# Mixture-of-experts stage after attention: rows of both choices are dispatched before the first expert tile, and first results return in 32 small pieces

## The chip, the cores and the metric

One core of a Trainium2 chip (trn2) runs the whole program. The metric is the device time of one execution in microseconds, as a median over runs. An execution under the hardware profiler gives the trace and has a time of its own.

## What is computed

The input is an image of 64 channels by 128 by 128 in float32. It is normalised along each row, goes through a gated attention layer with four heads (projection, softmax over the row, projection back) and is added to itself. Then each of the 8192 rows of 128 values is a token for a mixture of eight experts:

```python
def _L0_ffn_ref(x, Wg, bg, W1, b1, W2, b2):
    TOP_K = 2
    xf = x.reshape(-1, D)                        # 8192 tokens of D = 128
    gate_logits = xf @ Wg + bg
    top_w, top_i = jax.lax.top_k(gate_logits, TOP_K)
    top_w = jax.nn.softmax(top_w, axis=-1)
    w_dense = jnp.sum(jax.nn.one_hot(top_i, E, dtype=xf.dtype) * top_w[..., None], axis=1)
    out = jnp.zeros_like(xf)
    for e in range(E):
        h = jax.nn.gelu(xf @ W1[e] + b1[e], approximate=False)
        out = out + w_dense[:, e:e + 1] * (h @ W2[e] + b2[e])
    return out.reshape(B, L, D)
```

The tokens that enter are the layer-normalised rows, and the result is added to the rows themselves. Only the two chosen experts of a token count, so the kernel sends each token to two experts.

## The kernel before

**Up to the routing.** The first half of the span is the attention, which the change does not touch. Then VectorE (DVE) normalises the 64 rows that each partition holds into `pay` (L984), TensorE (PE) computes the gate logits, and VectorE works out for each choice k the row `pos[k]` at which each token goes (`route`, L1008). A token's payload is 128 values, its weight and its own number (528 bytes).

**Dispatch.** GpSimd (POOL) issues one indirect DMA per payload column: 128 tokens, one from each partition, are scattered to the buffer `routed[k]` in device memory (`scatter_rows`, L623). There are 64 of them for the first choice and 64 for the second. Both choices use the same `pay`; between them VectorE overwrites the weight column (L1091), which waits until the first 64 have landed and raises `meta_ready` to 2.

**Tiles.** Each choice is a slot of 39 tiles of 256 rows, sorted by expert, 78 tiles in all. Each tile goes through these steps: SyncE (SP) loads its rows (`load_rows`, L520, 132 KB) into one of 8 buffers; PE transposes them (L1304); ScalarE (ACT) and VectorE split them into a high and a low half-precision part (L792, L1099); PE multiplies by the first weights (L1314 to L1316); ACT applies the gelu (L801); VectorE splits its result (L1105, L1107); PE multiplies by the second weights (L1322 for the bias, L1330); ACT scales by the token's weight into `yo` (L809); POOL scatters the two halves of 128 rows to `expert_out[slot]` (`send_rows`, L627, two indirect DMAs at L630). The engines run staggered: in step s, PE transposes tile s+1, does the first products of tile s and the second products of tile s-1. The steps -1 to 4 are written out, the steps 5 to 44 are a loop of five iterations with eight steps in its body, the steps 45 to 76 a second loop of four iterations, and three steps are written out behind it (`tile_steps`, L386).

**Order on POOL.** All 64 first-choice scatters come first. Then, for each of the 39 tiles of slot 0, some second-choice scatters come ahead of `send_rows(t)`: eight ahead of tile 0, and from there 56 spread over 31 tiles, by this line:

```python
due = [LEAD + (HALF - LEAD) * t // (SLOT_TILES - 8) for t in range(SLOT_TILES)]
```

Slot 1 has the sends alone. `send_rows(t)` waits for `y_ready`.

**Order on SP.** SP waits until the first-choice scatters have landed, and issues the loads of slot 0. The load of tile t waits for the send of tile t-8, whose buffer it takes. Then SP waits for the second-choice scatters and loads the first eight tiles of slot 1. Once slot 0 is sent, it loads the first choice's results from `expert_out[0]` into `shared` in four chunks of 16 rows per partition, two DMAs of 512 KB each (L539), with eight tile loads between two chunks. VectorE adds them to `xt` four rows per partition at a time, once in every other step of the second loop (`add_first`, L1112), and waits for a chunk at its first quarter. After the last send come the second choice's results (L547, L1125) and the output (L551).

Of the kernel before, what the change touches and what calls it, by code (L numbers as in the profile page):

```python
# [50 lines left out]
def wait(engine, sem, value):  # L51

    if isinstance(value, int) and value <= 0:
        return
    engine.wait_ge(sem, value)
# [12 lines left out]

def build(nc, x, ln_w, ln_b, wq, wk, wv, wb, wg_w, wg_b, wrep_w, wrep_b, Wg, bg, W1, b1, W2, b2, out):
    _, C, H, W = x.shape  # L70
    NH = wb.shape[0]
    HC = wq.shape[0]
    D = HC // NH
    HALF = H // 2
    R = 4
# [3 lines left out]
    CH = 4  # L79
    CR = HALF // CH  # L80
    E, _, HID = W1.shape
    HB = HID // P
    TOKENS = C * H
    TILE = 256
    SLOT_TILES = TOKENS // TILE + E - 1
    TILES = 2 * SLOT_TILES
    ROW = W + 4
    IN_BUFS = 8
    YO_BUFS = 4
    B2_ROWS = 33  # L90
    WPIECE = E * HID // UNITS
    assert W == P and H == P and 2 * C == P and HC == P and UNITS % 2 == 0

    with ExitStack() as ctx:
        def sb(name, shape, dt=F32):
            return ctx.enter_context(nc.sbuf_tensor(name, shape, dt))
# [4 lines left out]
        def sem(name):  # L101
            return ctx.enter_context(nc.semaphore(name))
# [3 lines left out]
        shared = sb("shared", [P, HALF, W])  # L106
# [28 lines left out]
        b1_sb = sb("b1_sb", [P, E, HB])  # L135
        b2_row = sb("b2_row", [B2_ROWS, E * P])
        wg_sb = sb("wg_sb", [P, E])
# [69 lines left out]
        def sbm(name, shape, dt=F32):  # L207
            return ctx.enter_context(nc.sbuf_tensor(name, shape, dt))
# [3 lines left out]
        w_l = [sbm(f"w{n}_l", [P, E, HB, P], F16) for n in (1, 2)]  # L212
        b2_parts = sbm("b2_parts", [B2_ROWS, E, HB, P], F32R)
        ones_x = sbm("ones_x", [B2_ROWS, P], F32R)
        rows_all = sbm("rows_all", [P, IN_BUFS, 2, ROW])
# [20 lines left out]
        hl = [sbm(f"hl{p}", [P, HB, TILE], F16) for p in range(2)]  # L236
        yo = [sbm(f"yo{b}", [P, 2, P]) for b in range(YO_BUFS)]
        pay_place = pay[:].bitcast(I32)[:, :, W + 1]
# [87 lines left out]
        scattered = [sem(f"scattered{k}") for k in range(2)]  # L326
# [9 lines left out]
        y_full = sem("y_full")  # L336
        y_ready = sem("y_ready")
        y_sent = [sem(f"y_sent{b}") for b in range(YO_BUFS)]
        y0_in = sem("y0_in")
        y0_added = sem("y0_added")  # L340
        y_in = [sem(f"y_in{c}") for c in range(CH)]
        y_added = sem("y_added")
# [3 lines left out]
        lwv = ln_w.rearrange("c (f i) j -> f c i j", f=2)  # L346
        lbv = ln_b.rearrange("c (f i) j -> f c i j", f=2)
        outv = out[0].rearrange("c (f i) j -> f c i j", f=2)

        LEAD = 8  # L350

        def chunk(c):
            return slice(c * CR, (c + 1) * CR)
# [29 lines left out]
        BODY = 8  # L383
# [29 lines left out]
        def sent_count(b, t):  # L413

            return 32 * ((t - b) // YO_BUFS + 1) if t >= b else 0

# [50 lines left out]
        def _(sp):  # L467
# [29 lines left out]
            sp.wait_ge(const_ready, 1)  # L497
            for row in (0, B2_ROWS - 1):
                sp.dma_start(b2_row[row:row + 1, :], b2.rearrange("(o e) d -> o (e d)", o=1)).then_inc(small_in, 16)
# [13 lines left out]
            outputs_v = [e[0:TOKENS].rearrange("(c f i) w -> f c i w", f=2, i=HALF) for e in expert_out]  # L513

            def sent_through(t):

                for b in range(YO_BUFS):
                    wait(sp, y_sent[b], sent_count(b, t))

            def load_rows(t):  # L520
                slot, n = divmod(t, SLOT_TILES)
                wait(sp, y_sent[t % YO_BUFS], sent_count(t % YO_BUFS, t - IN_BUFS))
                sp.dma_start(rows_in[t % IN_BUFS], routed_v[slot][n]).then_inc(rows_loaded[t % IN_BUFS], 16)

            LATER = SLOT_TILES + IN_BUFS
            sp.wait_ge(scattered[0], 16 * HALF)
            for t in range(SLOT_TILES):
                load_rows(t)
            sp.wait_ge(scattered[1], 16 * HALF)
            for t in range(SLOT_TILES, LATER):  # L530
                load_rows(t)

            sent_through(SLOT_TILES - 1)
            for c in range(CH):
                if c:
                    for t in range(LATER + BODY * (c - 1), LATER + BODY * c):
                        load_rows(t)
                for f in range(2):
                    sp.dma_start(shared[f * C:(f + 1) * C, chunk(c), :], outputs_v[0][f, :, chunk(c), :]).then_inc(y0_in, 16)  # L539
            for t in range(LATER + BODY * (CH - 1), TILES):  # L540
                load_rows(t)

            sent_through(TILES - 1)
            sp.wait_ge(y0_added, HALF // R)
# [10 lines left out]
        def _(pool):  # L555
# [67 lines left out]
            def scatter_rows(k, i):  # L623
                pool.indirect_dma_start(routed[k], bass.IndirectOffsetOnAxis(ap=pos[k][:, i:i + 1], axis=0),  # L624
                                        pay[:, i, :], None).then_inc(scattered[k], 16)

            def send_rows(t):  # L627
                pool.wait_ge(y_ready, t + 1)
                for k in range(2):
                    pool.indirect_dma_start(  # L630
                        expert_out[t // SLOT_TILES],
                        bass.IndirectOffsetOnAxis(ap=row_place[t % IN_BUFS][:, k, W + 1:W + 2], axis=0),
                        yo[t % YO_BUFS][:, k, :], None).then_inc(y_sent[t % YO_BUFS], 16)

# [2 lines left out]
                scatter_rows(0, i)  # L637

            pool.wait_ge(meta_ready, 2)
            due = [LEAD + (HALF - LEAD) * t // (SLOT_TILES - 8) for t in range(SLOT_TILES)]  # L640
            for t in range(SLOT_TILES):
                for i in range(due[t - 1] if t else 0, min(HALF, due[t])):
                    scatter_rows(1, i)
                send_rows(t)
            for t in range(SLOT_TILES, TILES):
                send_rows(t)

        @block.scalar
# [169 lines left out]
        def _(dve):  # L818
            chain = Chain(dve, dve_step)

            for c in range(CH):
# [8 lines left out]
                k = chunk(c)  # L830
# [22 lines left out]
            for c in range(CH):  # L853
                k = chunk(c)
# [25 lines left out]
            for f in range(2):  # L880
                k = slice(f * C, (f + 1) * C)
# [194 lines left out]

            chain.link(nc.vector.tensor_scalar(b2_row[:], b2_row[:], hscale[0:B2_ROWS, 1:2], hscale[0:B2_ROWS, 2:3], ALU.mult, ALU.mult))
            b2_e = b2_row[:].rearrange("o (e d) -> o e d", e=E)
            chain.link(nc.vector.tensor_copy(b2_parts[:, :, 0, :], b2_e))
            lo = slice(B2_ROWS - 1, B2_ROWS)  # L1080
            chain.link(nc.vector.tensor_tensor(b2_parts[lo, :, 0, :], b2_e[lo], b2_parts[lo, :, 0, :], ALU.subtract))
# [29 lines left out]

            def add_first(g, j):  # L1112

                if j == 0:
                    dve.wait_ge(y0_in, 32 * g + 32)
                k = bass.ds(g * CR + j * R, R)
                nc.vector.scalar_tensor_tensor(xt[:, k, :], shared[:, k, :], y_scale[:, 0:1], xt[:, k, :],
                                               ALU.mult, ALU.add).then_inc(y0_added, 1)

            tile_steps(dve, tile_step, add_first)  # L1120

            dve.wait_ge(y0_added, HALF // R)
# [237 lines left out]
```

## Time and profile before

| what | value |
|---|---|
| runs | 1155.31 to 1161.32 us, median 1159.59 us (3 runs) |
| the profiled execution's own time | 1150.0 us |
| its span | 1148.2 us, mean granted TensorE clock 0.827 |
| PE, DVE, ACT, POOL busy | 62%, 66%, 54%, 39% of the span |
| bytes moved | 70.39 MB, mean 61 GB/s |
| chain that ended last | PE 35%, DVE 26%, issue 26%, ACT 4%, DMA 4% |

Times in the profile count from the start of the span. A row of a timeline is one instruction, or several merged, with its start, its length, and in brackets the idle time of its engine before it and what ended that. "issue" is idle time of an engine in which it waited for nothing that the profile shows; "remote" is a release that the profile can't place. PE is the multiplying, PEld the loading of weights into the array. The granted clock is a share of 2.4 GHz: 0.5 is 1.2 GHz.

### The profile page before, as it was taken

What the parts mean: (1) busy time and instruction counts of PE and PEld (TensorE: products, weight loads), DVE (VectorE), ACT (ScalarE), POOL (GpSimd) and SP (SyncE); (2) the same over time, 40 slices, a digit from 0 to 9 for tenths busy, and PEclk for the clock granted to TensorE, in tenths of its full rate; (3) what the DMA queues carried; (4) which work ended last, traced back from release to release, by engine and by line L of the source; (5) the groups of instructions that cost most, each with busy time, mean ns of one, the idle gap of its engine ahead of it and who ended that gap; (6) DMA issues with size and microseconds to landing.
All of it is one profiled execution on the core that took longest, in us unless ns stands there. A gap on an engine that the chain in (4) does not pass through costs nothing.

```text
span 1148.2 us, 24693 instructions
## 1 busy us (share of the span) xinstructions
PE 710.1 (62%) x7641; PEld 541.2 (47%) x7642; DVE 758.4 (66%) x2465; ACT 615.8 (54%) x1531; POOL 445.3 (39%) x492
## 2 busy tenths in 40 slices
PE   0036888888888888739500025757675777797760
PEld 0003666666666666625300014545554565676650
DVE  4795899999999999975484004334443455686653
ACT  0024898898888889816412014434443465576550
POOL 3001243434334343310058763555554643454350
PEclk9996899999999999958755556877787788898885
DMA  9735999900000000000001121211121213432219
GB/s 203 173 73 153 165 26 167 18 0 0 0 0 0 0 0 0 0 1 0 1 33 39 53 83 38 57 54 56 56 58 51 65 54 85 108 92 76 77 57 276
DMA packets 102861, 70.39 MB, mean 61 GB/s; under 512 B 52645, under 2 KB 93158, under 8 KB 99752
## 3 DMA queue, kind: packets, MB, share of 16 engines
q1 hardware_dynamic: 92392, 42.65, 24.5%
q0 software_dynamic: 9152, 18.89, 5.0%
q10 hardware_dynamic: 1280, 8.39, 3.2%
q8 instruction: 18, 0.29, 0.1%
q14 instruction: 19, 0.16, 0.1%
HBM read 36.04 MB, written 33.61 MB: 61 GB/s over the span
## 4 chain that ended last, share of the span: by engine, by line
PE 35%; DVE 26%; issue 26%; ACT 4%; DMA 4%; another core or an unknown queue 1%; POOL 1%; SPq 1%; DVEq 0%; ACTq 0%; POOLq 0%
PE PT L1330 11%; DVE L L919 6%; DVE pl L909 4%; PE S L1314 3%; PE S L1316 3%; PE S L1315 3%; PE PT L1322 2%; DMA xt<-in_x 2%; DVE rowstat L442 2%; DVE xt L944 2%; DMA shared<-expert_out 2%; PE S L1148 1%; PE A L1171 1%; PE PT L1196 1%
## 5 line engine op out<-in xcount | busy, mean ns | idle before, releaser
L630 POOL DMA_INDIRECT expert_out<-yo,rows_all x156 | 158.8, 1018 | 200.8 <-ACT yo L809 162.3
L801 ACT ACTIVATE hf<-S,b_sb,inv_hscale 128x256 f32<-128x256 f32 x312 | 153.7, 567 | 72.8 <-remote 42.8
L624 POOL DMA_INDIRECT routed<-pay,pos x128 | 132.3, 1034 | 121.4 <-DVE pay L1059 81.1
L712 ACT ACTIVATE L<-L,lmin 128x128 f32<-128x128 f32 x512 | 159.2, 390 | 0.4
L919 DVE CUSTOM_DVE_ANT_0 L<-S,biasN,logit_scale 128x128 f32<-128x128 f32 x512 | 148.4, 345 | 2.5 <-issue 1.9
L1105 DVE TENSOR_SCALAR hh<-hf,hscale 128x512 f16<-128x512 f32 x156 | 77.5, 497 | 87.9 <-ACT hf L801 64.5
L607 POOL TENSOR_TENSOR og<-gt,on 128x256 f32<-128x256 f32 x64 | 46.5, 727 | 229.3 <-DVE on L932 229.3
L1107 DVE SCALAR_TENSOR_TENSOR hl<-hf,hscale,hh 128x512 f16<-128x512 f32 x156 | 117.4, 753 | 5.6
L792 ACT ACTIVATE fx_h<-A 128x256 f16<-128x256 f32 x39 | 14.9, 383 | 183.3 <-PE A L1304 68.4
L1330 PE MATMUL PT<-w_h,hh 128*128 x624 | 91.6, 229 | 16.3 <-issue 10.7
L1304 PE MATMUL A<-identity,rows_all 128*128 128x128 f32 x78 | 18.3, 323 | 134.4 <-DMA rows_all<-routed 72.3
L1314 PE MATMUL S<-fx_h,w_h 128*128 128x256 f16 x312 | 97.9, 314 | 5.2 <-issue 4.9
L1330 PE MATMUL PT<-w_h,hl 128*128 x624 | 91.5, 228 | 13.7 <-issue 13.7
L1315 PE MATMUL S<-fx_l,w_h 128*128 128x256 f16 x312 | 98.1, 314 | 2.3 <-issue 2.3
L1316 PE MATMUL S<-fx_h,w_l 128*128 128x256 f16 x312 | 97.8, 313 | 1.5 <-issue 1.3
L1330 PE MATMUL PT<-w_l,hh 128*128 x624 | 90.5, 227 | 7.8 <-issue 7.8
L707 ACT ACTIVATE ph<-PT 128x512 f16<-128x512 f32 x128 | 76.0, 594 | 25.5 <-PE B L1213 13.3
L1099 DVE TENSOR_TENSOR fx_l<-A,fx_h 128x256 f16<-128x256 f32 x39 | 16.4, 422 | 104.1 <-ACT fx_h L792 66.1
L1196 PE MATMUL PT<-identity,L 128*128 128x128 f32 x512 | 83.0, 301 | 3.2 <-DVE pl L909 2.5
L909 DVE TENSOR_TENSOR pl<-PT,ph 128x512 f16<-128x512 f32 x128 | 82.8, 682 | 2.1 <-ACT ph L707 2.1
L1304 PEld LDWEIGHTS A<-identity,rows_all 128*128 128x128 f32 x78 | 9.0, 160 | 136.2 <-issue 136.1
L1196 PEld LDWEIGHTS PT<-identity,L 128*128 128x128 f32 x512 | 64.5, 155 | 8.1 <-DVE pl L909 2.9
(235 smaller groups left out, 2085.7 us busy)
## 6 DMA issues: line engine op xcount, KB each, us to landing
rows_all<-routed SPq DMA_DIRECT2D x78, 132.0 KB
routed<-blank SPq DMA_DIRECT2D x2, 5031.0 KB, 41.6
shared<-expert_out SPq DMA_DIRECT2D x16, 512.0 KB, 11.4
xt<-in_x SPq DMA_DIRECT2D x8, 512.0 KB, 24.6
shared<-in_L_conv_ln_w ACTq DMA_DIRECT2D x8, 512.0 KB, 11.8
shared<-in_L_conv_ln_b ACTq DMA_DIRECT2D x8, 512.0 KB, 10.4
out<-xt SPq DMA_DIRECT2D x8, 512.0 KB, 9.7
expert_out<-yo,rows_all POOLq DMA_INDIRECT x156
```

The costliest lines, as they stand in the source:

```text
L624: pool.indirect_dma_start(routed[k], bass.IndirectOffsetOnAxis(ap=pos[k][:, i:i + 1], axis=0), pay[:, i, :], None).then_inc(scattered[k], 16)
L630: pool.indirect_dma_start(expert_out[t // SLOT_TILES], bass.IndirectOffsetOnAxis(ap=row_place[t % IN_BUFS][:, k, W + 1:W + 2], axis=0), yo ...
L712: last = nc.scalar.activation(L[p][:, h, i, :], L[p][:, h, i, :], ACT.Exp, scale=-1.0, bias=lmin[p][:, h * R + i:h * R + i + 1])
L801: last = nc.scalar.activation(hf[p][:, b, :], S[2 * p + pair][:, k * TILE:(k + 1) * TILE], ACT.Gelu, scale=inv_hscale[:, 0:1], bias=b1_fla ...
L909: nc.vector.tensor_tensor(pl[i % 2][:], PT[i % 2][:], ph[i % 2][:], ALU.subtract).then_inc(pl_ready, 1)
L919: last = nc.vector.tensor_tensor_reduce(out=L[p][:, h, i, :], in0=S[h][:, i * P:(i + 1) * P], in1=biasN[:, h, :], scale=logit_scale[:, 0:1 ...
L1107: nc.vector.scalar_tensor_tensor(hl[p][:, b, :], hf[p][:, b, :], hscale[:, 2:3], hh[p][:, b, :], ALU.mult, ALU.subtract).then_inc(hl_ready, 1)
L1196: last = nc.tensor.transpose(PT[i % 2][:, h * P:(h + 1) * P], L[p][:, h, i, :], identity[:])
L1314: nc.tensor.matmul(dst, w1_h[:, block_at], fx_h[p][:], start=True, stop=False)
L1315: nc.tensor.matmul(dst, w1_h[:, block_at], fx_l[p][:], start=False, stop=False)
L1316: last = nc.tensor.matmul(dst, w1_l[:, block_at], fx_h[p][:], start=False, stop=True)
L1330: last = nc.tensor.matmul(PT[p][:, k * P:(k + 1) * P], h_part[p][:, b, k * P:(k + 1) * P], w_part[:, block_at], start=False, stop=b == HB ...
```

## The change

All 128 scatters are issued ahead of the first send, and SP waits for all of them before it loads the first tile. `LEAD` and `due` go. The four chunks of first results become 16 pieces of 4 rows per partition, two DMAs of 128 KB each. Piece g is issued behind the load of tile 46 + 2g, and waits until piece g-2 was added. VectorE waits for each piece.

```diff
+    FIRST_BACK = 46
...
-        y0_in = sem("y0_in")
+        y0_in = [sem(f"y0_in{k}") for k in range(2)]
...
-
-        LEAD = 8
...
-            LATER = SLOT_TILES + IN_BUFS
+            def load_first(g):
+                wait(sp, y0_added, g - 1)
+                for f in range(2):
+                    sp.dma_start(shared[f * C:(f + 1) * C, g * R:(g + 1) * R, :],
+                                 outputs_v[0][f, :, g * R:(g + 1) * R, :]).then_inc(y0_in[g % 2], 16)
+
             sp.wait_ge(scattered[0], 16 * HALF)
-            for t in range(SLOT_TILES):
+            sp.wait_ge(scattered[1], 16 * HALF)
+            for t in range(TILES):
                 load_rows(t)
-            sp.wait_ge(scattered[1], 16 * HALF)
-            for t in range(SLOT_TILES, LATER):
-                load_rows(t)
-
-            sent_through(SLOT_TILES - 1)
-            for c in range(CH):
-                if c:
-                    for t in range(LATER + BODY * (c - 1), LATER + BODY * c):
-                        load_rows(t)
-                for f in range(2):
-                    sp.dma_start(shared[f * C:(f + 1) * C, chunk(c), :], outputs_v[0][f, :, chunk(c), :]).then_inc(y0_in, 16)
-            for t in range(LATER + BODY * (CH - 1), TILES):
-                load_rows(t)
+                if t >= FIRST_BACK and (t - FIRST_BACK) % 2 == 0 and (t - FIRST_BACK) // 2 < HALF // R:
+                    if t == FIRST_BACK:
+                        sent_through(SLOT_TILES - 1)
+                    load_first((t - FIRST_BACK) // 2)
...
-            due = [LEAD + (HALF - LEAD) * t // (SLOT_TILES - 8) for t in range(SLOT_TILES)]
-            for t in range(SLOT_TILES):
-                for i in range(due[t - 1] if t else 0, min(HALF, due[t])):
-                    scatter_rows(1, i)
-                send_rows(t)
-            for t in range(SLOT_TILES, TILES):
+            for i in range(HALF):
+                scatter_rows(1, i)
+            for t in range(TILES):
                 send_rows(t)
...
             def add_first(g, j):
 
-                if j == 0:
-                    dve.wait_ge(y0_in, 32 * g + 32)
+                dve.wait_ge(y0_in[j % 2], 64 * g + 32 * (j // 2) + 32)
```

## Rows read from the trace of the kernel before

**Rows 1.** Stretches (columns: us; PE, PEld, DVE, ACT, POOL busy; clock; DMA; GB/s)
```profile
715.50:771.79 56.29, 36.12 (x313) 27.63 (x313) 22.03 (x40) 22.18 (x56) 30.75 (x32) 0.80 0.21 60
771.79:824.50 52.71, 36.53 (x312) 27.12 (x313) 23.33 (x40) 22.70 (x56) 30.27 (x30) 0.76 0.19 56
...
881.20:929.27 48.07, 34.23 (x312) 26.38 (x313) 23.31 (x40) 22.80 (x56) 24.58 (x24) 0.78 0.20 56
929.27:966.30 37.03, 28.71 (x312) 23.48 (x313) 22.03 (x40) 22.41 (x56) 15.92 (x16) 0.91 0.34 86
966.30:1002.56 36.26, 28.55 (x312) 23.72 (x313) 25.00 (x44) 22.63 (x56) 16.44 (x16) 0.88 0.36 90
1002.56:1039.18 36.62, 29.16 (x313) 24.32 (x313) 24.83 (x44) 22.63 (x56) 16.34 (x16) 0.87 0.33 87
1039.18:1074.81 35.63, 28.07 (x312) 23.43 (x313) 24.71 (x44) 22.63 (x56) 16.33 (x16) 0.93 0.35 89
```

**Rows 2.** Timeline of PE, two stops in a tile and one at a loop's head
```profile
707.07 0.22 PE L1330 MATMUL PT<-w_h,hl 128*128 x1 [1.09 <-issue]
708.47 0.27 PE L1330 MATMUL PT<-w_h,hl 128*128 x1 [1.18 <-issue]
...
966.30 0.69 PE L1304 MATMUL A<-identity,rows_all 128*128 128x128 f32 x2 [6.72 <-issue]
```

**Rows 3.** Timeline of POOL, first and last of a burst, and the last second-choice scatter
```profile
699.65 1.46 POOL L630 DMA_INDIRECT expert_out<-yo,rows_all  x1 [15.39 <-ACT yo L809]
...
707.73 0.95 POOL L624 DMA_INDIRECT routed<-pay,pos  x1 [0.30 <-issue]
...
909.15 0.96 POOL L624 DMA_INDIRECT routed<-pay,pos  x1 [0.30 <-issue]
```

**Rows 4.** Chain that ended last, in order of time, pieces of the loops (start, us)
```profile
936.30 1.45 PE PT L1330 x24
939.59 1.45 PE PT L1330 x24
...
1062.39 1.74 PE PT L1330 x24
1066.48 1.50 PE PT L1330 x24
```

**Rows 5.** Timeline of POOL, first-choice scatters and the eight behind them
```profile
582.94 1.11 POOL L624 DMA_INDIRECT routed<-pay,pos  x1 [81.09 <-DVE pay L1059]
...
609.92 5.20 POOL L624 DMA_INDIRECT routed<-pay,pos  x1 [0.30 <-issue]
...
671.57 0.96 POOL L624 DMA_INDIRECT routed<-pay,pos  x1 [0.30 <-issue]
674.40 0.96 POOL L624 DMA_INDIRECT routed<-pay,pos  x1 [1.87 <-issue]
...
683.23 1.03 POOL L624 DMA_INDIRECT routed<-pay,pos  x1 [0.31 <-issue]
```

**Rows 6.** Timeline of DVE, the rewriting of the weight column
```profile
673.90 0.22 DVE L1091 COPY pay<-weight 128x64 f32<-128x64 f32 x1 [55.21 <-DMA routed<-pay,pos]
```

**Rows 7.** Timeline of SP's queue
```profile
673.89 274.76 SPq L523 DMA_DIRECT2D rows_all<-routed  x47
...
1058.40 1.12 SPq L539 DMA_DIRECT2D shared<-expert_out  x2
```

**Rows 8.** Timeline of PE, the written-out steps
```profile
676.32 0.66 PE L1304 MATMUL A<-identity,rows_all 128*128 128x128 f32 x2 [72.27 <-DMA rows_all<-routed]
...
688.24 0.55 PE L1322 MATMUL PT<-b_parts,ones_x 33*128 x1 [4.39 <-issue]
692.20 0.39 PE L1330 MATMUL PT<-w_h,hh 128*128 x2 [3.41 <-DVE hl L1107]
```

**Rows 9.** Timeline of ACT, the second pair of tile 0's gelus
```profile
689.73 1.02 ACT L801 ACTIVATE hf<-S,b_sb,inv_hscale 128x256 f32<-128x256 f32 x2 [6.83 <-remote]
```

**Rows 10.** DMA issues of the page: size of one, median us to landing
```profile
shared<-expert_out SPq DMA_DIRECT2D x16, 512.0 KB, 11.4
```

## The prediction

> **What bounds the kernel now.** I read the chain of waits, then the table of stretches, then the timelines of PE and POOL. Only the expert stage, from 673.9 us, is touched. Its bulk is a loop whose iterations are eight steps, so the table cuts it at PE's first transpose of each iteration [rows 1]. All iterations have the same 312 or 313 matmuls, but the first takes 56.3 us, the second 52.7, the third again over 50 and the fourth 48.1, and the next four 37.0, 36.3, 36.6 and 35.6. The reader is to see what else differs: POOL has 24 to 32 instructions in the first four and 16 in the others, and the granted clock is 0.76 to 0.80 against 0.87 to 0.93. DMA moves more in the last four (86 to 90 GB/s against 56 to 60), so it is not bytes that slow the others.
>
> PE's timeline shows how the time goes: inside one group of products, where no wait on an engine stands, PE stops for 1.1 us at a time, put down to "issue" [rows 2]. Beside it lies POOL's timeline: from 699.65 to 708.7 it issues seven indirect DMAs with some 0.3 us between them, sends and scatters mixed, and the two stops fall at the end of that burst [rows 3]. With the last second-choice scatter at 909.15 [rows 3] the stops end, still in slot 0: the tiles behind it pass every 3.29 us [rows 4]. So the slowdown belongs to the second-choice scatters among the sends, not to slot 0, and PE is starved of instructions while POOL's DMAs stand close. That POOL's packets hold up PE's instruction fetch is my reading; the rows show only that both coincide.
>
> Ahead of the loop there is a second bound: VectorE stands 55.2 us for the first-choice scatters [rows 6]. They are serial on POOL [rows 5], and the first tile waits for them.
>
> **Part 1: the second scatters ahead of the tiles.** Before, the last first-choice scatter starts at 671.57, SP issues its first load at 673.89 (2.32 us later) and the first second-choice scatter starts at 674.40 [rows 5, 7]. The eight up to 683.23 start 8.83/7 = 1.261 us apart [rows 5]. After, 64 stand in a row: 63 x 1.261 = 79.5, so the last starts at 753.9 and has landed at 756.2. SP's first load moves from 673.9 to 756.2: **+82.3 us**. Nothing hides it: VectorE has nothing left to do ahead of the tiles but the weight column [rows 6], and every engine waits for the first tile. The first batch's pitch was (671.57 - 582.94)/63 = 1.407, because of a few long ones about 609.92 (5.20 us) [rows 5]; that would make this term 9.2 larger. I take 1.261, the pitch of the second-choice scatters themselves. No scatter comes closer, so the term's other end is 82.3 itself.
>
> **Part 2: the loop without scatters.** POOL has two sends per tile, as now in the last four iterations: 2 x 1.26 = 2.5 us in 3.29. The five iterations of the first loop take 966.30 - 715.50 = 250.8 us [rows 1]. The three of the second loop that the table ends on average 36.17; five of these are 180.9, so **-69.9 us**. By the shortest, 35.63, it would be -72.6; by the longest clean one, 37.03, -65.6. I take the mean, because each has one stop at the loop's head (6.72 us at 966.30 [rows 2]) that stays with or without scatters.
>
> **Part 3: the written-out steps.** PE starts at 676.32 and enters the loop at 715.50 [rows 1, 8]. The eight lead scatters (674.4 to 684.3 [rows 5]) fall on this start. Two stops of 1.09 and 1.18 us are of the kind found in the loop [rows 2]: 2.3 us go. Then PE stands 4.39 us on "issue" and 3.41 for VectorE, which waits for ACT, which stood 6.83 us between two pairs of gelus [rows 8, 9]. Without ACT's stop the second pair would follow at 682.9, VectorE's split would end at about 685.2, and PE would go on there and not at 692.2: 7.0 us. Whether this is the same starvation or first-pass code that is slow in any case no row tells. Bounds 2.3 and 9.3, the middle **-5.8 us**, since the rows near it speak for both.
>
> **Part 4: pieces for chunks.** The bytes are the same, and the last row loads and adds come in the same steps. A chunk disturbs the tile it falls on: the chunk at 1058.40 [rows 7] makes one tile 4.09 us and not 3.29 [rows 4], 0.8 us, and the second loop has three. Four pieces have the work of a chunk, so I take **0**; at best 3 x 0.8 = 2.4 are saved; at worst each of 16 pieces costs as a chunk does, 12.8 - 2.4 = +10.4. The new wait of SP (piece g waits for the add of piece g-2, VectorE's step 42 + 2g) holds back the row load of tile 47 + 2g, which PE transposes in step 46 + 2g: four steps, 13 us. Without it that load would wait for the send of tile 39 + 2g, which ACT writes in step 41 + 2g, so the new wait delays it by about one step. VectorE's wait for piece g comes in step 46 + 2g, also some 13 us behind its issue, and a pair four times as large lands in 11.4 us [rows 10]. Behind that wait stands the next tile's split, for which PE would wait. The 24 extra issues on SP and the 12 extra waits at the adds cost nothing, SP being idle between loads.
>
> The Trainium skill (DMA: Bandwidth & Descriptors, the measurements from device memory) has a rule against this part: put at least 1 MiB in a DMA to get 75% of peak. By that the 128 KB pieces are inefficient; the result would be the worst end just named. The row loads of 132 KB, one per 3.29 us without a wait on them in the last four iterations, speak against it here.
>
> **Sum**, against the profiled execution's own 1150.0 us: 82.3 - 69.9 - 5.8 + 0 = +6.6, so 1156.6. The median of the runs, 1159.59, lies 9.6 above that execution; the same difference on it gives **1166.2 us**. The tail (last results, last add, output) is unchanged. In short, most of what the interleaving costs now is what it hides: 75.7 us of slowdown against 82.3 of serial POOL time.
>
> **Rivals.**
> 1. Break-even. The price of starvation is all of what the bounds allow: 72.6 in the loop and 9.3 ahead of it, 81.9 together. Then 1159.6 + 0.4 = 1160.0. For it: a stop of both PE and ACT right at the lead scatters [rows 8, 9]. Against it: PE stops for 6.72 us at a loop's head without scatters too [rows 2].
> 2. Not slower but faster: ordinary runs starve more than the profiled one. The iterations with scatters differ by 4 us among themselves, those without by 1, so the 9.6 us between execution and median may lie there. If all of it does and goes, with break-even else: 1150.4. It decides once the runs' starvation exceeds the profiled by more than 6.2 us beyond rival 1. Against it: nothing locates the 9.6 us.
> 3. Pieces disturb one by one: the worst end of part 4, 1166.2 + 10.4 = 1176.6. For it: chunks do. Against it: row loads don't.
> 4. The pitch is 1.407 in the second batch as well: 1175.4.
> 5. The stops stay. The Trainium skill (Runtime: NRT & Kernel Launch, Instruction fetch mechanics) calls the crossing of an instruction block "mostly hidden". By that the 1.1 us stops would be something else, maybe slot 0's own. Worked out from rows: only +82.3 is left, 1241.9. The clean tiles of slot 0 behind 909 [rows 1, 4] speak strongly against it.
> 6. The change doesn't do what it says: the tiles would start before 756. SP's two waits at the head exclude it; no chance.
>
> **How the numbers follow.** Forecast 0.50, rival 1 0.22, rival 2 0.13, rival 3 0.07, rival 4 0.05, rival 5 0.03. A measurement of this kernel can tell about 0.5%, 5.8 us, from no change. The forecast's sum stands just past that bound (+6.6), and its terms spread by some 4 us either way, so of its 0.50 I give 0.34 to slower and 0.16 to same. Slower: 0.34 + 0.07 + 0.05 + 0.03 = 0.49. Same: 0.16 + 0.22 = 0.38. Faster: 0.13. The range runs from rival 2 to rival 3, 1150 to 1177; outside it lie rival 5 and the far parts of the others. The likeliest case's own range is 1161 to 1171.
>
> **What would show it.** First row load at 756 (part 1), scatters 1.26 us apart. Each iteration of the first loop at 35.6 to 37 us, with a clock near 0.9 and 16 POOL instructions (part 2). From PE's first transpose to the loop entry 30 to 37 us, not 39.2; ACT's stop of 6.8 us gone or not decides between forecast and rival 1 (part 3). No wait of VectorE on a DMA at the adds and iterations of the second loop at 36 (part 4). First load far from 756, or any first-loop iteration over 40 us, proves me wrong.

## The result and the profile after

The changed kernel takes 1176.07 us (median of 4 runs, 1173.98 to 1181.52), the kernel before beside it 1158.34 us (4 runs): ratio 1.016, 95% interval 1.0114 to 1.0207, so 1.6% slower. The forecast was slower, 1166.2 us in a range of 1150 to 1177.

The experiments will show that the answer depends on where a program runs. The kernel before took 1158 to 1161 us in the runs above and in one later set, 1154 in another, and 1068 in four other sets of runs, with no median between. A set's runs share one chip. I call the places with 1154 to 1161 **place A** and those with 1068 **place B**. What makes the difference no run tells. It may not be the chip alone: the second set of part 1 alone (place B, 1068.96) and, ten minutes later, the set of the last experiment (place A, 1153.79) bear the same chip number, 1; whether it names the same chip both times is not known.

The stretches of the expert stage after the change, cut as in [rows 1] at PE's first transpose of each iteration (columns: us, then busy time of PE, PEld, DVE, ACT, POOL with instructions, granted clock, DMA share, GB/s):

```profile
760.10:792.51 32.41, 21.23 (x173) 16.09 (x173) 14.42 (x26) 14.67 (x33) 5.83 (x6) 0.76 0.19 50
792.51:828.16 35.65, 28.91 (x312) 24.16 (x313) 22.63 (x40) 22.73 (x56) 16.53 (x16) 0.88 0.21 58
828.16:862.91 34.75, 28.40 (x313) 23.58 (x313) 22.45 (x40) 22.62 (x56) 16.15 (x16) 0.89 0.22 62
862.91:897.39 34.48, 27.98 (x313) 23.43 (x313) 22.48 (x40) 22.62 (x56) 16.17 (x16) 0.90 0.22 62
897.39:933.60 36.21, 29.35 (x312) 24.57 (x313) 22.49 (x40) 22.68 (x56) 16.14 (x16) 0.88 0.22 63
933.60:969.39 35.79, 28.43 (x312) 23.59 (x313) 22.71 (x40) 22.63 (x56) 16.21 (x16) 0.93 0.24 70
969.39:1010.14 40.75, 30.42 (x312) 24.45 (x313) 24.67 (x44) 22.09 (x56) 16.49 (x16) 0.88 0.29 78
1010.14:1051.51 41.37, 30.43 (x313) 24.61 (x313) 24.67 (x44) 22.08 (x56) 16.20 (x16) 0.87 0.27 75
1051.51:1092.04 40.53, 30.17 (x312) 24.40 (x313) 24.68 (x44) 22.09 (x56) 16.47 (x16) 0.88 0.28 79
```

The reader is to see two things. The five iterations of the first loop are at 34.5 to 36.2 us with 16 POOL instructions each, where the first four took 48.1 to 56.7. And the second loop, which before took 35.6 to 36.6 [rows 1], now takes 40.5 to 41.4, although DVE and ACT are busy for about the same time as before and PE for only 1.7 us more (30.3 for 28.6).

SP's queue after the change:

```profile
757.81 195.25 SPq L522 DMA_DIRECT2D rows_all<-routed  x47
953.23 1.15 SPq L527 DMA_DIRECT2D shared<-expert_out  x2
...
988.97 1.09 SPq L527 DMA_DIRECT2D shared<-expert_out  x2
990.11 2.24 SPq L522 DMA_DIRECT2D rows_all<-routed  x2
997.97 1.09 SPq L527 DMA_DIRECT2D shared<-expert_out  x2
```

The first row load stands at 757.81, not 673.89 [rows 7]. In the second loop each piece is issued with two row loads right behind it. What follows one such issue on ACT and VectorE, from the timelines of the two:

```profile
989.13 0.69 ACT L802 ACTIVATE yo<-PT,rows_all 128x128 f32<-128x128 f32 x2
993.49 0.38 ACT L785 ACTIVATE fx_h<-B 128x256 f16<-128x256 f32 x1 [3.67 <-remote]
...
993.91 0.42 DVE L1092 TENSOR_TENSOR fx_l<-B,fx_h 128x256 f16<-128x256 f32 x1 [2.27 <-ACT fx_h L785]
```

PE's transposes into B, for which this split waits, start at 989.75 and take 0.39 us in its timeline, so by the records ACT could go on at about 990.2. It goes on at 993.49. VectorE does not wait for a DMA anywhere in the second loop, so the pieces are not late; something holds up ACT behind them, and PE stops too, for less:

```profile
993.42 0.28 PE L1322 MATMUL PT<-w_h,hl 128*128 x2 [0.49 <-issue]
```

**The account by stages**, after minus before, in the profiled executions (1172.6 and 1148.2 us of span):

| stage | before | after | difference | predicted |
|---|---|---|---|---|
| first scatter to first row load | 582.94 to 673.89 | 584.43 to 757.81 | +82.4 | +82.3 |
| start of the stage | 582.94 | 584.43 | +1.5 | 0 |
| load to first transpose | 2.4 | 2.3 | -0.1 | 0 |
| written-out steps | 39.2 | 32.4 | -6.8 | -5.8 |
| first loop | 250.8 | 176.9 | -73.9 | -69.9 |
| three iterations of the second loop | 108.5 | 122.7 | +14.1 | 0 |
| from its fourth to the end | 73.4 | 80.6 | +7.2 | 0 |

The sum is +24.4. The medians differ by 17.7: the profiled execution of before (1150.0) was quicker than its median by 8.3, that of the changed kernel (1174.39) by 1.7.

### The profile page after: what moved, and what is told of

Its sections match the earlier page's. It is cut to its first block, busy times and chain, and to the rows that moved or that the text cites. A ratio compares the mean times of both kernels' runs of the same rounds, so it can differ in the third digit from the quotient of the medians.

```text
span 1172.6 us, 24721 instructions
## 1 busy us (share of the span) xinstructions
PE 686.3 (59%) x7641; PEld 531.4 (45%) x7642; DVE 758.2 (65%) x2465; ACT 614.3 (52%) x1531; POOL 444.2 (38%) x492
## 4 chain that ended last, share of the span: by engine, by line
issue 54%; PE 21%; SPq 11%; DVE 4%; DMA 4%; ACT 2%; another core or an unknown queue 2%; ACTq 0%; POOL 0%; POOLq 0%
PE PT L1322 8%; SPq L506 4%; PE S L1308 3%; SPq L508 3%; PE S L1306 3%; PE S L1307 3%; DMA xt<-in_x 2%; ACT hf L794 2%; PE PT L1314 2%; DMA shared<-expert_out 1%; SPq L494 1%; PE S L1140 1%; DVE x L825 1%; PE A L1296 1%
## 5 line engine op out<-in xcount | busy, mean ns | idle before, releaser
L1306 PE MATMUL S<-fx_h,w_h 128*128 128x256 f16 x312 | 91.9, 295 | 1.5 <-DVE fx_l L1092 0.6
L1308 PE MATMUL S<-fx_h,w_l 128*128 128x256 f16 x312 | 91.6, 293 | 1.0 <-issue 1.0
L1307 PE MATMUL S<-fx_l,w_h 128*128 128x256 f16 x312 | 91.8, 294 | 0.0
L1322 PE MATMUL PT<-w_h,hl 128*128 x624 | 88.9, 226 | 3.2 <-issue 3.2
```

The costliest lines, as they stand in the source:

```text
L1306: nc.tensor.matmul(dst, w1_h[:, block_at], fx_h[p][:], start=True, stop=False)
L1307: nc.tensor.matmul(dst, w1_h[:, block_at], fx_l[p][:], start=False, stop=False)
L1308: last = nc.tensor.matmul(dst, w1_l[:, block_at], fx_h[p][:], start=False, stop=True)
L1322: last = nc.tensor.matmul(PT[p][:, k * P:(k + 1) * P], h_part[p][:, b, k * P:(k + 1) * P], w_part[:, block_at], start=False, stop=b == HB ...
```

## The experiments

**One part at a time, and two variations.** The first kernel has part 1 (all scatters first) without part 4:

```diff
             sp.wait_ge(scattered[0], 16 * HALF)
+            sp.wait_ge(scattered[1], 16 * HALF)
             for t in range(SLOT_TILES):
                 load_rows(t)
-            sp.wait_ge(scattered[1], 16 * HALF)
...
-            due = [LEAD + (HALF - LEAD) * t // (SLOT_TILES - 8) for t in range(SLOT_TILES)]
...
+            for i in range(HALF):
+                scatter_rows(1, i)
+            for t in range(TILES):
+                send_rows(t)
```

> All scatters ahead of the tiles, but the first results still return in four chunks of two 512 KB DMAs at their old places. Theory A (the pieces cost what the second loop lost: its iterations went from 36.2 to 40.9 us, 21 us in all with the written-out end): second loop back at 36 to 37 us per iteration, the time about 1155 us, near the kernel before, with the first loop staying at 35 to 36 us. Rival (the second loop is slower for another reason, such as when the stage starts): the time stays near 1176.

The second has the pieces of the change, and POOL's order and SP's waits for the scatters as before.

> Scatters interleaved as before, but the first results return in 32 pieces. Theory A: the second loop goes from 36.2 to about 41 us per iteration, the first stays at 48 to 56, and the time is about 1158 + 20 = 1178 us. Rival: 1158.

The third frees SP from the wait:

```diff
-        y0_in = [sem(f"y0_in{k}") for k in range(2)]
+        y0_in = [sem(f"y0_in{k}") for k in range(4)]
...
-                wait(sp, y0_added, g - 1)
+                wait(sp, y0_added, g - 3)
...
-                dve.wait_ge(y0_in[j % 2], 64 * g + 32 * (j // 2) + 32)
+                dve.wait_ge(y0_in[j], 32 * g + 32)
```

> The changed kernel, its pieces as small as before, but each waits for the add four pieces back and not two, so that SyncE is no longer held behind it. Theory H (the wait holds SyncE, so that two pieces and two row loads are issued in one knot, 520 KB in 3.4 us, behind each add): knots go, second loop back at about 36.5 us, time near 1157. Theory S (the small size of the pieces itself disturbs, wherever they stand): second loop stays at 40 to 41 us, time near 1176.

The fourth is the kernel before with `LEAD = 36`.

> The kernel before with 36 and not 8 second-choice scatters ahead of tile 0, and 28 spread over 31 tiles. The head grows by 28 x 1.262 = 35.3 us in every theory. Theory P (PE starves in proportion to the scatters between the sends): half of the 74 us that the first loop lost comes back, the time stays at 1158 plus or minus 5. Theory B (PE starves only when seven or more of POOL's DMAs stand in a row, because POOL is behind): the first loop comes down to 37 to 40 us per iteration, and the time to 1125 to 1140.

Measured, all at place B, where the kernel before took 1067.72 us (14 runs):

| kernel | median us | ratio to before | 95% interval |
|---|---|---|---|
| part 1 alone | 1136.94 | 1.0662 | 1.0628 to 1.0696 |
| part 4 alone | 1067.80 | 1.0005 | 0.9982 to 1.0028 |
| pieces not held | 1136.66 | 1.0661 | 1.0629 to 1.0694 |
| 36 scatters first | 1073.73 | 1.0068 | 1.0039 to 1.0096 |

None of the expected times was met, because all of them took the price of starvation to be the kernel's own. At B it is nearly nothing. Stretches of part 4 alone, whose scatters are interleaved as in the kernel before:

```profile
677.16:703.91 26.75, 18.82 (x173) 14.40 (x173) 14.18 (x26) 14.59 (x33) 16.49 (x18) 0.82 0.29 84
703.91:738.99 35.08, 28.63 (x313) 23.92 (x313) 22.02 (x40) 22.79 (x56) 23.80 (x24) 0.89 0.24 70
738.99:774.90 35.91, 28.42 (x312) 23.56 (x313) 22.38 (x40) 22.79 (x56) 27.40 (x28) 0.93 0.29 81
774.90:813.76 38.86, 29.59 (x313) 24.36 (x313) 22.44 (x40) 22.78 (x56) 29.72 (x31) 0.90 0.28 77
813.76:853.76 40.00, 28.97 (x313) 23.71 (x313) 23.44 (x40) 22.78 (x56) 30.56 (x32) 0.93 0.28 81
...
888.74:923.64 34.90, 28.38 (x313) 23.66 (x313) 24.55 (x44) 22.79 (x56) 16.26 (x16) 0.89 0.34 93
```

and of part 1 alone:

```profile
759.68:786.48 26.80, 18.65 (x173) 14.39 (x173) 14.18 (x26) 14.58 (x33) 5.76 (x6) 0.82 0.24 61
786.48:821.20 34.72, 28.49 (x313) 23.77 (x313) 22.06 (x40) 22.78 (x56) 15.77 (x16) 0.89 0.22 63
...
890.33:924.47 34.14, 27.88 (x312) 23.41 (x313) 21.84 (x40) 22.78 (x56) 15.84 (x16) 0.90 0.22 63
...
958.51:992.96 34.45, 27.91 (x312) 23.41 (x313) 24.24 (x44) 22.79 (x56) 16.06 (x16) 0.90 0.38 94
992.96:1028.63 35.67, 29.30 (x312) 24.57 (x313) 24.39 (x44) 22.79 (x56) 15.94 (x16) 0.88 0.34 89
```

An iteration with 24 POOL instructions takes 35.1 us at B and took 48.1 at A [rows 1]; one without scatters takes 34.0 to 34.7 at B and 34.5 to 36.2 at A. So in the loops the places differ where POOL has scatters between the sends, and hardly elsewhere. The written-out steps are an exception: without scatters they take 32.4 us at A and 26.8 at B. What slows part 4 alone at B is POOL itself: 32 instructions at 1.26 us are 40.3 us, just the 40.00 of that iteration, and PE then waits for rows whose buffer a late send still holds:

```profile
799.83 0.44 PE L1301 MATMUL A<-identity,rows_all 128*128 128x128 f32 x2 [1.85 <-DMA rows_all<-routed]
```

The account at B, part 1 alone against part 4 alone (the kernel before has no trace from there): the head costs the same 82 us (the first load moves from 674.83 to 757.39), the written-out steps give nothing back (26.8 us with the eight scatters beside them and without), and the first loop falls from 184.8 to 172.0 (703.91 to 888.74, 786.48 to 958.51), 12.8 us. 82.6 - 12.8 is 69.8, and the medians differ by 69.1. The pieces cost nothing: 34.4 to 34.9 us with them and 34.5 to 35.7 with chunks.

The kernel with 36 ahead shows an error in its own expectation: scatters ahead of send 0 do not delay tile 0, since SP waits for the first choice alone. They delay the sends. PE works through the eight tiles whose rows are loaded and then stands, since the next load waits for a late send:

```profile
PE A L1304 <- DMA rows_all<-routed: 15.1, 1, 15.1
```

**Which place, which ratio.** Both kernels unchanged, in one set:

> The kernel before once more, for a trace beside the following run on the same chip. The first four experiments ran where the kernel before took 1068 us and not 1158. Theory C (how far PE starves behind POOL's DMAs depends on the chip that runs the program): the time is either about 1068 with first-loop iterations near 35 to 40 us, or about 1158 with iterations of 48 to 56; nothing between. Rival (it varies from one execution to the next): some other time and a mix of iterations.

> The changed kernel once more, beside the kernel before on the same chip. Theory C: if the kernel before is at 1068, nothing starves, so the scatters' 82 us at the head come back to nothing and the pieces cost nothing: about 1137, 6.5% slower. If it is at 1158, about 1176, 1.6% slower. Rival (starvation is the kernel's alone): 1.6% slower in either case.

The kernel before took 1160.77 us (7 runs) and the changed one 1175.64: ratio 1.0135, interval 1.0078 to 1.0192. Place A again, with the starvation in the traced execution of before:

```profile
772.47:830.78 58.31, 39.47 (x313) 28.18 (x313) 22.35 (x40) 22.21 (x56) 30.13 (x31) 0.73 0.19 54
...
1016.42:1053.42 37.00, 28.54 (x312) 23.55 (x313) 24.49 (x44) 22.52 (x56) 16.26 (x16) 0.92 0.33 86
```

and 40.2, 39.3 and 39.7 us in the second loop of the changed one. The times fall on two levels and not on a spread, as theory C had it; that it is the chip that decides, as theory C also had it, isn't shown.

This second pair of traces from A, spans of 1166.2 and 1170.0 us, splits its difference otherwise than the first:

| stage | first pair, after minus before | second pair |
|---|---|---|
| start and head, up to the first transpose | +83.8 | +81.4 |
| written-out steps | -6.8 | -8.9 |
| first loop | -73.9 | -80.3 |
| second loop and what follows | +21.3 | +11.5 |
| sum | +24.4 | +3.7 |

So one pair of executions doesn't fix the size of a term at A. Scatters among the tiles cost 80.7 us in one and 89.1 in the other, and the pieces 21.3 and 11.5. The medians, 17.7 and 14.9 apart, lie between the two sums. A second run of part 1 alone, of the 36 and of the pieces not held was meant for A and fell on B.

> All scatters ahead of the tiles, first results in four chunks at their old places. Where the kernel before takes about 1160: theory A (the pieces cost the second loop 21 us) gives about 1155 with second-loop iterations of 36 to 37 us; the rival (part 1 alone costs it) gives 1176 with 41. Where the kernel before takes about 1068: again 1137.

> 36 second-choice scatters ahead of tile 0, 28 spread over 31 tiles. Where the kernel before takes about 1160: theory P (starvation in proportion to the scatters that are left) about 1160, theory B (starvation only in long bursts of POOL) 1125 to 1140. Where it takes 1068: again about 1074.

> The changed kernel with SyncE not held by the add two pieces back. Where the kernel before takes about 1160: theory H (SyncE's knot of four DMAs behind each add stops ACT) about 1157 with second-loop iterations of 36 to 37; theory S (small pieces disturb wherever they stand) about 1176 with 41. Where it takes 1068: again 1137.

They repeat their first runs: 1138.46 (ratio 1.0646), 1075.58 (1.0056) and 1137.81 us (1.065) beside 1068.96.

**One kernel, different iterations.** To get several answers from one execution, the scatters and pieces were distributed unevenly. Of the kernel with free pieces, the first form is:

```diff
-                wait(sp, y0_added, g - 3)
+                if g < 6:
+                    wait(sp, y0_added, g - 1)
+                elif g < 12:
+                    wait(sp, y0_added, g - 3)
+                else:
+                    sp.wait_ge(y0_in[g % 4], 96)
...
+            ahead = [40] + [0] * 2 + [0, 1] * 4 + [1] * 8 + [1, 2] * 4
+            due = [min(HALF, sum(ahead[:t + 1])) for t in range(SLOT_TILES)]
+            for t in range(SLOT_TILES):
+                for i in range(due[t - 1] if t else 0, due[t]):
+                    scatter_rows(1, i)
+                send_rows(t)
```

with pieces 12 to 15 all issued behind the load of tile 70, and SP waiting for the second scatters only ahead of tile 39.

> One kernel whose iterations differ, read iteration by iteration. Second-choice scatters: 40 ahead of tile 0, then 4, 8, 12, 0, 0 in the five iterations of the first loop. First results: pieces 0 to 5 with SyncE held by the add two back (as in the changed kernel), 6 to 11 with the add four back (never holding), 12 to 15 issued together. Where the kernel before takes about 1160: theory P (1.4 us of starvation per interleaved scatter) gives 47 us for the iteration with 8 and 52 for that with 12, over 35.6; theory B (POOL only hurts when it can't keep up, above some 12 scatters per iteration) gives 36 and 36 to 40. Theory H (holding makes the knot) gives 41 us for the first iteration of the second loop and 36 to 37 for the second; theory S (the pieces themselves) 41 for both. The first iteration of the first loop holds a stop of PE while POOL catches up with its 40 scatters, and tells nothing. Where the kernel before takes about 1068, all stay at 34 to 36.

> The mixed kernel once more. Where the kernel before takes about 1160: theory P (1.4 us of starvation per interleaved scatter) gives 47 us for the first-loop iteration with 8 scatters and 52 for that with 12, over 35.6 without; theory B (POOL only hurts when it can't keep up) gives 36 and 36 to 40. Theory H (holding SyncE makes the knot) gives 41 us for the first iteration of the second loop and 36 to 37 for the second; theory S (the pieces themselves) 41 for both. Where the kernel before takes about 1068, all as in the first run of it.

Both runs fell on B: 1079.08 and 1079.6 us, 1.0% and 1.2% above before. At B iterations with 24 or 25 POOL instructions took 35.5 and 34.9 us, and PE stood once for 20.2 us while POOL caught up with its 40. The last kernel has

```diff
-            ahead = [40] + [0] * 2 + [0, 1] * 4 + [1] * 8 + [1, 2] * 4
+            ahead = [16] + [0] * 2 + [2] * 16 + [1] * 16
```

> As the mixed kernel, but with 16 second-choice scatters ahead of tile 0, then 16, 16, 8, 8, 0 in the five iterations of the first loop. Pieces 0 to 5 held by the add two back, 6 to 11 not held, 12 to 15 together. Where the kernel before takes about 1068: POOL needs 32 x 1.262 = 40.4 us for an iteration with 16 and 30.3 for one with 8, against 34.5 of PE, so it falls 6 us behind in each of two iterations, PE waits for row loads for some of that, and the time is 1068 to 1074. Where it takes about 1160: theory P gives 58 us for the iterations with 16 and 47 for those with 8, theory B 50 to 58 and 36; theory H 41 then 36 in the second loop, theory S 41 and 41.

It fell on place A: 1155.3 us (10 runs), ratio 1.0012 (0.9982 to 1.0041) to 1153.79. Its stretches:

```profile
719.51:776.88 57.37, 38.10 (x313) 27.91 (x313) 23.55 (x40) 22.67 (x56) 32.34 (x32) 0.71 0.19 54
776.88:833.59 56.71, 38.94 (x313) 28.73 (x313) 22.02 (x40) 22.34 (x56) 30.57 (x31) 0.74 0.20 58
833.59:878.31 44.72, 32.08 (x312) 25.18 (x313) 22.90 (x40) 22.56 (x56) 24.71 (x24) 0.84 0.21 59
878.31:927.37 49.06, 34.54 (x312) 26.83 (x313) 22.10 (x40) 22.34 (x56) 22.95 (x23) 0.78 0.19 53
927.37:964.88 37.51, 29.18 (x313) 23.91 (x313) 22.03 (x40) 22.45 (x56) 15.89 (x16) 0.91 0.26 74
964.88:1004.99 40.11, 29.81 (x313) 23.96 (x313) 24.57 (x44) 22.12 (x56) 16.45 (x16) 0.88 0.28 77
1004.99:1044.24 39.25, 29.80 (x312) 24.36 (x313) 24.49 (x44) 22.24 (x56) 16.33 (x16) 0.89 0.34 92
1044.24:1082.88 38.64, 28.90 (x313) 23.56 (x313) 24.49 (x44) 22.24 (x56) 16.40 (x16) 0.90 0.32 89
```

*Scatters.* The iterations with 16 take 57.0 us on average, those with 8 take 46.9. Over the 35.4 of a clean one in the changed kernel (176.9 / 5) that is 21.6 / 16 = 1.35 and 11.5 / 8 = 1.44 us per scatter. The spread is wide: the two iterations with 8 give 1.17 and 1.71, and over this kernel's own iteration without scatters (37.5 us, with two pieces in it) the averages are 1.22 and 1.17. In the kernel before, the first four iterations had 16, 14, 15 and 8 scatters and gave 1.31, 1.24, 1.42 and 1.59 each. Theory P (in proportion) gave 58 and 47; theory B (only when POOL can't keep up) gave 36 for the iterations with 8. P holds, B falls: with 24 x 1.26 = 30.3 us of POOL in 46.9 there is room, and PE is slowed all the same. Only a part of the price is PE standing still. With 16 scatters PE is busy for 38.5 us and stands for 18.5; in a clean iteration of the changed kernel it is busy for 28.6 and stands for 6.8. So some 12 of the 21.6 us are stops. In some 10 PE is busy for longer on the same 312 or 313 matmuls, beside a granted clock of 0.71 to 0.74 and not 0.88 to 0.93. Whether the clock fell because of the stops, no run tells.

*Pieces.* The iteration with held pieces takes 40.1 us, the one with pieces not held 39.2, the one in which four come together 38.6. SP's queue has 4, 5 and 5 pieces in these three stretches, so over the 35.4 of a clean iteration a piece costs 1.2, 0.8 and 0.6 us. Theory H asked for 36 to 37 without the hold and theory S for 41; neither is met. Most of the loss stays without the hold, so in this execution it is not the main cause, but per piece it may add a third; iterations of one kind differ by 0.8 us among themselves (40.5 to 41.4), so one of each doesn't settle the share. The changed kernel has two pieces of its own that no add holds, 0 and 1, in the last iteration of its first loop. That iteration takes 35.8 us in one trace and 37.4 in the other, against 35.3 for the four ahead of it: 0.3 and 1.1 us per piece, where the held ones of the same traces cost 1.4 and 1.1. The share of the hold stays open. Stops of ACT like that of the changed kernel (some 3.5 us, put down to "remote") stand twice in the stretch with held pieces and once in each of the two others, as here:

```profile
1032.08 0.38 ACT L797 ACTIVATE fx_h<-A 128x256 f16<-128x256 f32 x1 [3.49 <-remote]
```

## Why the prediction was right, and which term was mis-sized

**Direction and range** were right: slower, 1176 in 1150 to 1177, but near its upper end. By medians the change cost 17.7 us, not 6.6. That the result lies inside the range is in part luck. The forecast carried the 9.6 us between the profiled execution of before and its median over to the changed kernel, whose own difference was 1.7; and parts 2 and 3 gave back 5.0 us more than forecast. Without these two, the error of part 4 alone would have led past 1177.

**Part 1** was right to 0.1 us: 82.4 for 82.3, at the pitch of 1.261 (82.7 in the second pair). Rival 4, a pitch of 1.407, fell.

**Part 2** gave 73.9 for 69.9. The clean iterations were at 35.4 rather than 36.2 us; the three of before from which I took the mean each hold a chunk and four adds. That the slowdown belongs to the second-choice scatters is now shown at place A: in a kernel that differs from before in their number per iteration it falls from 21.6 to 11.5 us when they fall from 16 to 8. That it is PE's instruction fetch that they hold up, as I read it, is not shown. Parts 2 and 3 together gave back 80.7 us in the first pair, nearer to rival 1's 81.9 than to my 75.7, and 89.1 in the second. That speaks for the premise of rival 2 as well: of the 18.0 us by which the second trace of before is longer than the first, 9.8 lie in the written-out steps and the first loop. It was part 4 that kept the result from break-even.

**Part 3** gave 6.8 for 5.8. At A, ACT's stop of 6.83 us between tile 0's gelus [rows 9] went with the eight scatters. At B the written-out steps take 26.8 us with or without them, so that stop was no first-pass cost of the program in itself. But 5.6 of the 12.4 us between A and B in these steps stayed at A without scatters (32.4 against 26.8), and no run tells why.

**Part 4** is the term that failed: 0 was taken, and the second loop and what follows it lost 21.3 us, twice the worst end of 10.4 (11.5 us in the second pair, just past it). The step that was wrong is "Four pieces have the work of a chunk, so I take 0"; its bound, "each of 16 pieces costs as a chunk does", was too low as well. What the prediction worked out about the waits held: no wait on a piece stands in the second loop. What it left out is that SP, held by the new wait, issues two row loads right behind each piece. The three iterations of the second loop went from 36.2 to 40.9; against 35.4 for the first loop that is 5.5 us for four pieces and their adds, 1.4 each (1.1 in the second pair), where a chunk of four times the bytes costs 0.8. This was rival 3, at 7%. The Trainium skill's rule against small DMAs (DMA: Bandwidth & Descriptors, the measurements from device memory) points this way at A; at B the pieces cost nothing (1.0005), so the rule doesn't settle it. It is a rule for the speed of the transfers themselves, and here the pieces were in time and other engines stood. That part 4 is the cause at A rests on two things. It is all that differs in that loop, and the first loop of the same execution is clean. And the uneven kernel, which has pieces but leaves 48 scatters among the tiles, loses there too: its three iterations of the second loop take 118.0 us, those of before 108.5 and 111.6, those of the changed kernel 122.7 and 119.2. Part 1 alone was never run at A.

**The sum at the two places.** A scatter costs 1.26 us ahead of the tiles. Among them the 64 cost 80.7 us in the first pair from A and 89.1 in the second, 1.26 and 1.39 each, so the move of all 64 is close to neutral there (82.4 - 6.8 - 73.9 = +1.7, and in the second pair 82.7 - 8.9 - 80.3 = -6.5), and the loss is part 4. At B it costs nothing until POOL is full, so the move costs 69 us, all of the loss. The forecast rested on one trace from A and would have been far off at B, where the changed kernel with chunks, or with pieces not held, is 6.5 to 6.6% slower; as it stands it was not run there.

**What stays open.** What held up PE and ACT at A. PE stands on "issue" inside a group of products, and a scatter costs about one POOL pitch, while 16 sends per iteration cost nothing that can be seen; a scatter's rows are 528 bytes and a send's 512, and no run tells number from size. The Trainium skill (Runtime: NRT & Kernel Launch, Instruction fetch mechanics) says that a taken branch outside the window forces a fetch, and PE's 5 to 8 us on "issue" at each loop's head, at A and at B, fit that, though no trace shows the fetch; that block crossings are "mostly hidden" fits B and the clean iterations at A, but not PE's stops beside scatters, if these are fetches. Nor is it known what makes a place A or B. No version beat the kernel before at either place: the closest are part 4 alone (1.0005 at B) and the uneven kernel (1.0012 at A).

## What to carry to other kernels

An operation's price beside other work must be compared with its price alone: at A a hidden scatter cost the tiles 1.26 to 1.39 us, about its own 1.26, at B nearly nothing, and moving it out of hiding is a gain only beyond that price. When a stall is put down to "issue" or "remote" beside DMA traffic, run both kernels at more than one place before you trust the ratio: here it was 1.3 to 1.6% at one, and its main part alone 6.6% at the other. And splitting one 512 KB return into four 128 KB ones was not free for the other engines at A, though no piece was late; at B it was.

## What the runs showed that I had not expected

- The same program took 1154 to 1161 us in some sets of runs and 1068 in others, 8% apart, and nearly all of it in one stage: the written-out steps (39.2 against 26.8 us) and the loop iterations with scatters (48 to 58 against 35 to 40); the figures of the faster place are those of part 4 alone, whose time there is that of the kernel before.
- At place A each interleaved scatter of 128 rows cost the tiles about 1.2 to 1.4 us, roughly in proportion from 8 to 16 per iteration, partly as stops of PE and partly as a lower granted clock.
- Two traces of the same two kernels at place A put the price of the same part at 21.3 and at 11.5 us.
- At place B POOL stood at 45 indirect DMAs in one iteration, and PE's only large stop besides the loop's head was a wait for row loads (20.2 us).
